# Cross-attention and mixture FFN on one core: q of the later blocks made from x as loaded, scaled by VectorE

## The reference

```
n   = layernorm(x)                                   # (x - mean) / sqrt(var + 1e-5), per token
q   = n @ wq + bq ; k = ctx @ wk + bk ; v = ctx @ wv + bv     # 16 heads of 8
o   = softmax((q k^T * 8**-0.5) v, over the 8 features of a head)   # no softmax over tokens
x1  = x + o @ wo^T + bo
t   = rmsnorm(layernorm(x1)) * norm_w
for each token the 2 best of 8 experts by t @ gate^T, weighted by softmax:
  h1, h3 = t @ w1^T + 2 * (t @ a1^T) @ b1^T , the same with w3, a3, b3   # 512 wide, rank 16
  act    = silu(h1) * h3
  y     += weight * (act @ w2^T + 2 * (act @ a2^T) @ b2^T)
out = x1 + y
```

## Time and profile before

| what | value |
|---|---|
| median of 3 runs | 298.84 us |
| lowest and highest run | 298.49 us, 299.08 us |
| profiled execution: span, first to last instruction | 296.7 us |
| its time over the span (median less span) | 2.1 us |
| instructions | 4518 |
| busy: TensorE | 287.4 us (97%) |
| busy: VectorE | 221.4 us (75%) |
| busy: ScalarE, POOL | 187.5 us, 187.0 us (63% each) |
| mean granted clock of TensorE | 0.992 of full speed |

### The profile page before, as it was taken

How to read it: one execution, slowest core, us unless ns; L and a number is a source line. 1 busy time by engine, 2 the same in 40 slices (tenths; PEclk the granted TensorE clock), 3 DMA queues, 4 the chain that set the end, 5 groups by cost and what they waited for, 6 DMA issues and landing times. The chain is left out here.

```text
span 296.7 us, 4518 instructions
## 1 busy us (share of the span) xinstructions
PE 287.4 (97%) x1487; PEld 238.4 (80%) x1487; DVE 221.4 (75%) x607; ACT 187.5 (63%) x310; POOL 187.0 (63%) x186
## 2 busy tenths in 40 slices
PE   8779999999999999999999999999999999999995
PEld 6557888878888888888888888888888887878874
DVE  3878986995689658894589765895579965795295
ACT  1467967674945966757755868459656658655532
POOL 3375599288970889419990589608982389518930
PEclk9979999999999999999999999999999999999999
DMA  5720020200220021200211011200012000200002
GB/s 147 287 66 9 0 73 1 72 1 11 97 73 0 0 72 38 71 1 2 71 50 60 0 49 59 71 0 2 1 37 73 0 0 35 75 1 0 0 2 71
DMA packets 7225, 12.45 MB, mean 42 GB/s; under 512 B 1825, under 2 KB 3234, under 8 KB 7202
## 3 DMA queue, kind: packets, MB, share of 16 engines
q1 hardware_dynamic: 6768, 11.77, 12.0%
q10 hardware_dynamic: 434, 0.39, 0.4%
HBM read 10.03 MB, written 2.13 MB: 41 GB/s over the span
## 5 line engine op out<-in xcount | busy, mean ns | idle before, releaser
L989 ACT ACTIVATE silu<-h_ps 128x512 f32<-128x512 f32 x64 | 37.4, 596 | 31.4 <-PE h_ps L641 29.8
L1639 POOL TENSOR_TENSOR um_lo<-umf,um_hi 128x1024 fp32r<-128x1024 f32 x7 | 16.9, 2414 | 60.5 <-ACT um_hi L981 60.5
L641 PE MATMUL h_ps<-um_hi,b_hi 128*128 128x512 f32 x128 | 51.4, 401 | 0.0
L641 PE MATMUL h_ps<-um_lo,b_hi 128*128 128x512 f32 x128 | 50.3, 393 | 0.5 <-DVE um_lo L1309 0.5
L641 PE MATMUL h_ps<-um_hi,b_lo 128*128 128x512 f32 x128 | 49.9, 390 | 0.0
L1322 DVE TENSOR_TENSOR act_first<-silu,h_ps 128x512 f32<-128x512 f32 x32 | 21.4, 680 | 20.9 <-ACT silu L989 16.1
L1322 DVE TENSOR_TENSOR act_second<-silu,h_ps 128x512 f32<-128x512 f32 x32 | 21.7, 679 | 16.6 <-PE h_ps L641 14.7
L1661 POOL TENSOR_TENSOR scaled<-act_second,ratio 128x512 f32<-128x512 f32 x24 | 31.5, 1313 | 1.3 <-DVE act_second L1322 1.3
L641 PEld LDWEIGHTS h_ps<-um_lo,b_hi 128*128 128x128 f32 x128 | 24.0, 188 | 6.9 <-DVE um_lo L1309 1.4
L981 ACT CAST um_hi<-umf 128x1024 fp32r<-128x1024 f32 x14 | 14.8, 1055 | 23.2 <-DVE umf L1303 22.2
L641 PEld LDWEIGHTS h_ps<-um_hi,b_lo 128*128 128x128 f32 x128 | 24.1, 188 | 4.5
(11 more groups left out here) (278 smaller groups left out, 789.2 us busy)
## 6 DMA issues: line engine op xcount, KB each, us to landing
chosen<-choice_dram SPq DMA_DIRECT2D x7, 512.0 KB, 3.6
x_in<-in_x_dram SPq DMA_DIRECT2D x7, 256.0 KB, 2.9
ctx_in<-in_ctx_t_dram SPq DMA_DIRECT2D x7, 256.0 KB, 3.2
out_dram<-y SPq DMA_DIRECT2D x7, 256.0 KB, 2.0
act_second<-in_hidden_w_dram SPq DMA_DIRECT2D x1, 512.0 KB, 4.1
act_second<-in_lora_w_dram SPq DMA_DIRECT2D x1, 512.0 KB, 5.6
v_parts<-in_down_w_dram SPq DMA_DIRECT2D x1, 512.0 KB, 5.3
ctx_in<-in_ctx_t_dram ACTq DMA_DIRECT2D x2, 128.0 KB, 3.2
```

What stands on the lines that cost most here:

```text
L641: mm = nc.tensor.matmul((h1_ps, h3_ps)[s][n % 2][:], b13[w][:, s, c * P:(c + 1) * P], um[k][m][:, s, :], start=False, stop=(i == 2), skip_ ...
L989: nc.scalar.activation(silu[:, n % SILU_RING, :], h1_ps[n % 2][:], ACT.Silu).then_inc(silu_done.sem, 1)
L1639: nc.gpsimd.tensor_tensor(um[1][1][:], umf[1][:], as_f32(um[1][0][:]), ALU.subtract)\
```

## The change

From block 2 on, x is no longer normalised and turned on the chip for q. The host passes x a second time, turned (`x_t`), and it is loaded straight into `xn_t`. Centring is a matrix (identity less 1/128, `center`), which TensorE multiplies once into wq (`center_queries`, into `wqc_sb`), ahead of `turn_x(1)`. q is then `wqc` times x as loaded, and must still be multiplied per token with rstd, which now runs along the columns: POOL makes rstd alone (`turned_rstd`), SP writes it to DRAM and reads it back to all partitions (`spread_rstd`), VectorE multiplies (`scale_queries`, from odd_ps into `q_t`), and ScalarE adds the bias in place (`bias_queries`). `turn_tok`, which needs odd_ps, waits for VectorE (`q_scaled`) in place of ScalarE. Blocks 0 and 1 make q as before.

```
+        rstd_rows = sb("rstd_rows", [P, BLK])
+        wqc_sb = sb("wqc_sb", [P, P])
+        center_sb = umf[0][:, 0, 0:P]
+        xt_in = xn_t[:]
+        rstd_dram = nc.dram_tensor("rstd_dram", (2, P * TILES), F32).ap()
...
+            def load_xt(n):
+                sp.wait_ge(q_mm.sem, q_mm.of(n - 1))
+                sp.dma_start(xt_in, x_t[:, n * BLK:(n + 1) * BLK]).then_inc(xt_loaded, 16)
+
+            def spread_rstd(n):
+                sp.wait_ge(rstd_done.sem, rstd_done.of(n))
+                sp.dma_start(rstd_dram[n % 2].rearrange("(p c) -> p c", c=TILES), rstd[:]).then_inc(rstd_out, 16)
+                sp.wait_ge(rstd_out, turned(n, 16))
+                if n > AHEAD:
+                    sp.wait_ge(q_scaled, turned(n - 1))
+                sp.dma_start(rstd_rows[:], rstd_dram[n % 2].partition_broadcast(P)).then_inc(rstd_in, 16)
...
+            load_xt(2)
+            spread_rstd(2)
             for b in range(BLOCKS):
                 if b + 3 < BLOCKS:
                     load_x(b + 3)
                     load_ctx(b + 3)
+                    load_xt(b + 3)
                 if b > 0:
                     store(b - 1)
                 if b + 1 < BLOCKS:
                     spread_choice(b + 1)
+                if b + 3 < BLOCKS:
+                    spread_rstd(b + 3)
...
             def turn_x(n, i=WHOLE):
...
+                else:
+                    pe.wait_ge(wqc_done, 1)
...
+            def center_queries():
+                pe.wait_ge(center_in, 16)
+                nc.tensor.matmul(h1_ps[0][:, 0:P], center_sb, wq_sb, start=True, stop=True).then_inc(wqc_mm, 1)
+
+            def turned_queries(n):
+                if n == AHEAD:
+                    pe.wait_ge(umf_done.sem, umf_done.of(0))
+                else:
+                    pe.wait_ge(o_t_done.sem, o_t_done.of(n - 3))
+                pe.wait_ge(xt_loaded, turned(n, 16))
+                nc.tensor.matmul(odd_ps[:], wqc_sb[:], xt_in, start=True, stop=True).then_inc(q_mm.sem, 1)
...
                 elif n + 1 < BLOCKS:
-                    pe.wait_ge(q_t_done.sem, q_t_done.of(n + 1))
+                    pe.wait_ge(q_scaled, turned(n + 1))
...
+            def centered_queries():
+                sc.wait_ge(wqc_mm, 1)
+                nc.scalar.copy(wqc_sb[:], h1_ps[0][:, 0:P]).then_inc(wqc_done, 1)
+
+            def bias_queries(n):
+                sc.wait_ge(q_scaled, turned(n))
+                nc.scalar.activation(q_t[:], q_t[:], ACT.Identity, bias=bq_sb[:, 0:1]).then_inc(q_t_done.sem, 1)
...
+            def scale_queries(n):
+                ve.wait_ge(q_mm.sem, q_mm.of(n))
+                ve.wait_ge(rstd_in, turned(n, 16))
+                nc.vector.tensor_tensor(tile4(q_t), tile4(odd_ps), rstd_rows[:].rearrange("q (p c) -> q c p", c=TILES),
+                                        ALU.mult).then_inc(q_scaled, 1)
...
+            def turned_rstd(n):
+                pool.wait_ge(mv_done.sem, mv_done.of(n))
...
+                nc.gpsimd.tensor_tensor(var_eps[:], mv[:, :, 1], eps_ln[:], ALU.add).then_inc(var_done.sem, 1)
+                pool.wait_ge(var_done.sem, var_done.of(n))
+                nc.gpsimd.tensor_tensor(rstd[:], var_eps[:], minus_half[:], ALU.pow).then_inc(rstd_done.sem, 1)
```

More of the change, by code:

```diff
@@ L86, in upto, with build_program @@
     return None if i is WHOLE else i + 1
-def build_program(nc: bass.Bass, x, ctx_t, wkv, query_w, mask_w, attn_w, rows, hidden_w, lora_w, down_w, b2, row_expert, out):
+def build_program(nc: bass.Bass, x, x_t, center, ctx_t, wkv, query_w, mask_w, attn_w, rows, hidden_w, lora_w, down_w, b2, row_expert, out):
     with ExitStack() as ctx:
@@ L258, in build_program @@
         ctx_first = [sem("ctx_first0"), sem("ctx_first1")]
+        center_in = sem("center_in")
+        wqc_mm = sem("wqc_mm")
+        wqc_done = sem("wqc_done")
         const_pool = sem("const_pool")
@@ L278, in build_program @@
         xn_done = signal("xn_done", first=2)
+        xt_loaded = sem("xt_loaded")
+        rstd_out = sem("rstd_out")
+        rstd_in = sem("rstd_in")
+        q_scaled = sem("q_scaled")
         ctx_hi_done = signal("ctx_hi_done")
@@ L390, in build_program, with turned @@
         PARTS = (slice(0, 2), slice(2, 3), slice(3, 4))
+        def turned(n, k=1):
+            return k * (n - AHEAD + 1)
         LAST = BLOCKS - 1
@@ L503, in keys_values @@
                         pe.wait_ge(masks_done.sem, masks_done.of(0))
-                else:
-                    pe.wait_ge(xn_t_done.sem, xn_t_done.of(n))
+                elif n == AHEAD:
+                    pe.wait_ge(ratio_done.sem, ratio_done.of(0))
                 for j in range(2):
@@ L765, in _ @@
             keys_values_ahead(1, 1)
+            center_queries()
             turn_x(1)
@@ L782, in _ @@
             first_base(0, 1)
-            turn_x(2)
             first_base(1, 0)
@@ L786, in _ @@
             hidden(0, 1)
-            queries(2)
+            turned_queries(2)
             turn_heads(1)
@@ L822, in _ @@
                 if early:
-                    turn_x(b + 2)
                     keys_values(b + 2, 0)
@@ L830, in _ @@
                 if early:
-                    queries(b + 2)
+                    turned_queries(b + 2)
                 tail(b - 1)
@@ L1033, in _ @@
             normal_x(1)
+            centered_queries()
             weight_high(B13, lora_w_in, b13, b13_raw)
@@ L1047, in _ @@
             exp_gap(0)
-            normal_x(2)
             first_ratio()
@@ L1062, in _ @@
             weight_high(B2, b2_in, b2_split, b2_raw[:])
-            queries(2)
+            bias_queries(2)
             silu_step(0, 3)
@@ L1094, in _ @@
                 output_t(b - 1)
-                if early:
-                    x_turned(b + 2)
                 b_high(b, 0)
@@ L1099, in _ @@
                 if early:
-                    queries(b + 2)
+                    bias_queries(b + 2)
                 silu_step(b, 4)
@@ L1467, in _ @@
             act_step(0, 1)
+            scale_queries(2)
             residual(1)
@@ L1512, in _ @@
                     keys_values(b + 2, 0)
+                    scale_queries(b + 2)
                 finish(b - 1)
@@ L1602, in rstd_x @@
                 inverse_root(mv, var_eps, neg_mean, rstd, shift, var_done, rstd_done, shift_done, n, eps_ln)
+            def turned_rstd(n):
+                pool.wait_ge(mv_done.sem, mv_done.of(n))
+                if n == AHEAD:
+                    pool.wait_ge(xn_done.sem, xn_done.of(n - 1))
+                else:
+                    pool.wait_ge(rstd_out, turned(n - 1, 16))
+                nc.gpsimd.tensor_tensor(var_eps[:], mv[:, :, 1], eps_ln[:], ALU.add).then_inc(var_done.sem, 1)
+                pool.wait_ge(var_done.sem, var_done.of(n))
+                nc.gpsimd.tensor_tensor(rstd[:], var_eps[:], minus_half[:], ALU.pow).then_inc(rstd_done.sem, 1)
             def rstd_x1(n):
@@ L1695, in _ @@
             ctx_low(2)
-            rstd_x(2)
+            turned_rstd(2)
             low(WKV, wkv_split, wkv_sb)
@@ L1710, in _ @@
             ctx_low(3)
-            rstd_x(3)
+            turned_rstd(3)
             um_low(1)
@@ L1764 @@
         "x": a["x"].transpose(1, 0, 2).reshape(SEQ, BATCH * D),
+        "x_t": a["x"].transpose(2, 0, 1).reshape(D, BATCH * SEQ),
+        "center": np.eye(D, dtype=np.float32) - np.float32(1.0 / D),
         "ctx_t": a["ctx_1024"].transpose(2, 0, 1).reshape(D, BATCH * SEQ),
```

18 lines of the change are left out of this document (5 added, 13 removed).

## The result

| | before | changed |
|---|---|---|
| median of the runs, us | 298.68 (298.49 to 299.08, 4 runs) | 302.85 (301.78 to 303.69, 4 runs) |
| ratio | | 1.0140 [1.0124, 1.0156] |
| profiled execution, span, us | 296.7 | 301.3 |
| TensorE busy | 287.4 (97%) | 289.2 (96%) |
| VectorE / ScalarE / GpSimd busy | 221.4 / 187.5 / 187.0 | 226.6 / 175.5 / 184.3 |

What follows compares the result with a forecast made beforehand. TensorE, 97% busy, was taken as the bound. Start and block 0 +0.38, block 1 -0.06, blocks 2 to 5 +0.48, together +0.80 on 298.84: 299.6 us; range over all cases 297.6 to 300.5 (forecast's own 299.0 to 300.5).

Steps and rivals of the forecast that it cites:

- The new wait: TensorE waits before turn_tok for VectorE's scale of q, taken as 1.18 us: 0.37 us in blocks 1 to 5 each.
- Four transposes less: TensorE turns less per block: 0.43 us saved in block 1, 0.25 us kept in each of blocks 2 to 5.
- Rival 1: Strided operand not slow, scale 0.69 us, TensorE doesn't wait before turn_tok: sum -1.05 us, 297.8 us; chance 0.22.
- The start: Centring product and copy delay turn_x(1), queries(1) and block 0's tokens by about 0.5 us; +0.38 taken, ends -0.12 and +0.6.
- the step "Nothing": In block 0, scale ahead of residual(1) delays POOL's chain; TensorE's 0.32 us wait for um_lo takes it up: no cost.
- What costs nothing: ScalarE's and POOL's dropped work is not waited for, and rstd's DRAM trip has a block's lead: no cost.
- Rival 2: Scale takes 0.95 us, TensorE waits 0.14 us in five blocks: 298.5 us; chance 0.13.
- Rival 3: All six blocks' savings of 0.43 us reach the end, 2.6 us less: 296.2 us; chance 0.06.
- Rival 4: TensorE waits for rstd's row or x turned, up to 3.6 us in each of five blocks: some 310 us; chance 0.04.

Runs made afterwards that it cites:

- run 3: Changed kernel with the row of rstd written tile by tile, so VectorE reads it at unit stride: 301.31 us, ratio 1.0112.
- run 11: Changed kernel with centring and block 2's scale late, unit stride from block 3, rstd write held until the choice landed, spare ScalarE copy, inputs last: 297.15 us, 0.9974.
- run 1: Kernel before with the two new inputs declared in second and third place but never loaded: 299.02 us, ratio 1.0043.
- run 5: Kernel before, unchanged, repeated for its start: no wait at the first key product, heads of block 0 at 15.39 us.
- run 9: Kernel before with the two new inputs declared last and never loaded: 298.14 us, ratio 1.0001.
- run 10: Changed kernel with its two new inputs declared last: 301.51 us, ratio 1.0101.
- run 4: Changed kernel with block 2's scale placed behind residual(1), moments_x1(1) and act_step(0, 2), its bias behind normal_tok(1): 300.51 us, ratio 1.0101.
- run 8: Changed kernel with centring product late, b2 cast behind its copy, block 2's scale behind residual(1), unit-stride rstd from block 3: 303.79 us, ratio 1.0183.
- run 6: Changed kernel with a spare 128x512 ScalarE copy where block 0's copy of x turned had stood: 299.19 us, ratio 1.0047.

## Why the prediction was wrong, and where it was right

**The new wait: right.** The scale instruction takes 1.086 us (taken 1.18; 0.69 and 1.18 were the ends) and costs 0.32 us a block (0.37); run 3, with the stride alone changed, has a period 0.35 us shorter. By the sentence of the Trainium skill on 4 fp32 (SBUF — State Buffer, section on the DMA port swizzle) it would have been 0.69 us; that is what run 11 measures at unit stride, so a step of 16 bytes is not free here. The section's other rule, at least two hits per line for full speed, fits the 1.086 us.

**Four transposes less: right in kind.** 0.30 us earlier at project (0.25), 0.18 left at the q product. Four periods +0.55 us against +0.48 predicted; that the sum comes so close is in part luck, as wait and saving are both some 0.05 us smaller than taken. Block 1, up to its turn_tok, gained 0.21 us in place of 0.06. Rival 1 is the same sum with p = 0.69, -0.25 a block; run 11 has -0.21.

**The start: mis-sized, and incomplete.** Counted from the heads, the centring's +0.5 us at first_base became +0.66 and the +0.38 at the first um_lo product +0.57, within the end of +0.6. But "The start" has no term for the load of what was there already: it puts that at nothing. The first loads came 0.5 us later because of the new inputs' place (runs 1, 5, 9, 10), and in the profiled execution a second stretch at half clock followed, 1.6 us more. Together +2.09 us at the heads. The second stretch does not come in every execution: the one run of the changed kernel at 0.994 is 1.0 to 1.9 us shorter than its three at 0.989. The trace of before held a hint: the first key product started straight behind the warm-up, with nothing in hand.

**Block 0: the step "Nothing" failed, twice.** The first time in its reasoning. It said that a TensorE kept back by the scale ahead of `residual(1)` would make this up in its wait of 0.32 us for um_lo. But that wait is *for VectorE*, on which the scale stands too: it has no room for work put on VectorE, it says that VectorE is the late one. The wait still stands at 0.32 to 0.41 us in every kernel here, and 0.41 us (run 4) of the scale's place went straight through; run 8, which besides other repairs has the scale late, is 0.33 us below run 6. The second time in "What costs nothing": ScalarE's lost copy is waited for by nobody, true, but its time had kept um_hi, and with it VectorE, off the port that POOL's heads needs. That is 0.63 us (run 6). Run 8, with the scale late and POOL first, has block 0 at 31.01: port and place together make 0.96 of the 1.24 us.

**Rivals 2 and 3** were not seen: the operand's price is near the upper end, and project does wait for heads_t in the later blocks. **Rival 4, a late transfer,** did not happen in the changed kernel: the row of block 2 is sent at 31.91 and used at 41.75. With the slower write a transfer was late in run 3 (the row, once) and in run 8 (the choice, twice). Its sum doesn't come out: five times 3.6 us is 18 us, some 317 us and not 310. Nor do the stated ends of the range follow from their terms, which give 299.1 to 300.2.

What stays open: why the place of unread inputs moves the landing of others (they may lie at other addresses in DRAM, but no run shows addresses), what brings the early fall of the clock in some executions and not in others (runs 4 and 6 have no fall at all, though TensorE idles 1.80 and 2.05 us ahead of the heads there), 0.3 us of block 0 that remain in run 8 (31.01 against 30.73), and the +0.40 us behind turn_tok of block 5.

## What to carry to other kernels

When work is taken off an engine that is not the bottleneck, list what that engine will now release earlier, and what two others will then start at the same time; for um_lo on VectorE and heads on GpSimd the first to start kept its short time in twelve profiles, and two ties went two ways. A bottleneck engine's wait for X is no slack for X. Cut both timelines at the same dozen instructions before explaining a difference: here the first quarter of the time held five sixths of the loss. Where the first loads are just in time, declare new inputs last.

## What was not expected of the hardware

- Two inputs declared and never read, in second and third place, made the first loads land 0.5 us later (first key product 4.86 to 5.14 us in nine profiles, 4.38 and 4.52 without them); declared last they left it at 4.38 to 4.42. How the place does this is open.
- VectorE's um_lo, 128x1024, and POOL's heads, 128x512, took 1.16 and 1.92 us or 1.94 and 1.08 us, by which started first; a tie (starts within 0.01 us) went one way in one execution and the other way in another.
- A write of 512 single words took 8.1 to 9.1 us (medians of runs 3, 8 and 11) in place of 3.3. A broadcast sent 0.36 us before it landed after some 9 us in place of 3.5 twice in run 8 and never in run 3; that the write held it up is not shown.
